# Products of constants in seven waits of TensorE: what they do to a block of four attention and feed-forward layers

## The chip, the cores and the metric

The kernel runs on one core of a Trainium2 chip. The metric is the device time of one execution in microseconds. Before the change three runs took 1488.58, 1493.6 and 1497.57 us, median 1493.6.

## The reference, cut to what matters

The reference takes x of shape (2, 1024, 256) in float32 and adds eight gated sub-layers to it, one after the other. Each reads the layer-normalised x of the one before:

```python
x = x + tanh(g_xattn[0]) * L0_xattn(layernorm(x), ctx, ...)   # A: 16 heads over 77 context rows
x = x + tanh(g_ffn[0])   * L0_ffn(layernorm(x), ...)          # B: GELU feed-forward, quantised weights, LoRA
x = x + tanh(g_xattn[1]) * L1_xattn(ctx, layernorm(x), ...)   # C: local attention
x = x + tanh(g_ffn[1])   * L1_ffn(layernorm(x), ...)          # D: windowed attention, routed heavy attention
x = x + tanh(g_xattn[2]) * L2_xattn(layernorm(x), ctx, ...)   # E: similarity x . ctx, softmax both ways
x = x + tanh(g_ffn[2])   * L2_ffn(layernorm(x), ...)          # F: gated recurrence over the 2 batch rows
x = x + tanh(g_xattn[3]) * L3_xattn(layernorm(x), ctx, ...)   # G: 16 heads again, with a bias and a mask
x = x + tanh(g_ffn[3])   * L3_ffn(layernorm(x), ...)          # H: 16 experts, 4 of them for each row
```

The change touches E, F, the start of G and H. In E the similarity of each of 2048 rows with 77 context rows goes through a softmax, weighs the context, and a second softmax over the rows gives one mean row for each of the two batches. F has two steps; the state of the first begins as a constant vector. In H a router picks 4 experts for each row, and each expert is a gated SiLU layer of 128 units.

## The kernel before, in words

Everything is float32 and stands in SBUF: x is 16 tiles of 128 rows by 256 columns, HT = 8 tiles for each of the B = 2 batches. PSUM is one tensor `ps` of 8 banks of 512 float32 values in each of 128 partitions. Each engine has one instruction stream written out by hand; semaphores order the streams. An engine works strictly in its written order, so a product that stands ahead of a wait is done whether or not the wait is over. There is no planner.

A layer ends with `x_new`: VectorE adds the layer's output to x and counts each tile on that semaphore. The next layer begins with `norm_dve` and `norm_act` (mean and variance by VectorE, the square root by ScalarE, lines 656 to 676).

Layer E on TensorE is `sim_pe`. Its steps, with the line that the profile gives each:
- It waits for E_step 1 (VectorE has made RT, line 1194) and makes a row of 154 numbers in bank 7 (line 1053).
- For n = 0 to 7, `turn_x(n)` transposes two tiles of normalised x into bank 0 or 1 (line 1063), ScalarE copies them out (line 1177), and `similarity(n)` multiplies them with RT (line 1072). VectorE takes the first four similarities at once (`largest(0)`, line 1214).
- `turn_a(0)` and `turn_a(1)` transpose the softmax weights (line 1081), ScalarE copies them (line 1185), and `weigh(0)`, `weigh(1)` multiply them with the context (line 1088).
- `from_weighed(0, b)` is lines 1098 and 1102, `batch_mean` lines 1117, 1120 and 1125, `from_x` line 1107. Then tiles 1 to 7 follow in the same way.

Layer F on TensorE is `rnn_pe`. It waits for x_new of E, though its first twelve products, one column each with a weight of 128 by 128, read only constants (line 1306). VectorE waits for them at line 1422, makes the biases and only then norms x (`norm_dve`, line 1434). `turn_x(0)` transposes four tiles (line 1321, copies line 1388), `from_x` is line 1328.

Layer G is `heads16_pe` with L = "G": after the wait for x_new of F come the keys of the context (line 298), its values (line 305), `turn_x(0)` (line 315) and `queries(0)` (line 325). VectorE spreads the keys at line 526.

Layer H is `moe_pe`. The router's tables end with products of one-hot matrices in float16 (line 2434). VectorE turns the result into addresses (line 2594), GpSimd gathers the rows of each of NJ = 80 tiles by indirect DMA (line 2676), and TensorE does for each tile `turn_rows` (line 2443), `gate_up` (line 2451), `turn_act` (line 2459) and `down` (line 2465). GpSimd's gathers of the expert outputs and the last sums follow when all 80 tiles are done.

The profile records one product of float32 matrices as two instructions MATMUL: the twelve products of line 1306 are its 24. A transposition is recorded as one.

Of the kernel before, what the change touches and what calls it, by code (L numbers as in the profile page):

```python
# [111 lines left out]
def nth(i, per, k):  # L112

    return i * per + (k + 1)
# [28 lines left out]
def done(layer, name):  # L143

    total = 0
    for each, count in TOTALS[name].items():
        if each == layer:
            return total
        total += count


def build(nc, ins, out):
    ctx = ExitStack()
    with ctx:
# [5 lines left out]
        def sem(name):  # L160
            if name not in sems:
                sems[name] = ctx.enter_context(nc.semaphore(name))
            return sems[name]
# [28 lines left out]
        packs, pk = {}, {}  # L192
# [9 lines left out]
        ps = ctx.enter_context(nc.psum_tensor("ps", [P, 8, 512], F32))  # L202
        ident = pk["const"]["ident"]
# [27 lines left out]

        block = ctx.enter_context(nc.Block())


        UNITS = [(b, c) for b in range(B) for c in range(DC)]
        NU = len(UNITS)
# [811 lines left out]
        def sim_pe(pe):  # L1048
            w = pk["E"]
            pe.wait_ge(sem("E_in"), LOADS["E"])  # L1050
            pe.wait_ge(sem("E_step"), 1)
            for c in range(DC):
                mm = nc.tensor.matmul(ps[:, 7, 0:B * SC], w["w2"][:, c:c + 1].to_broadcast([P, P]), ctxT[:, c, :],
                                      start=c == 0, stop=c == DC - 1)
            mm.then_inc(sem("E_row_ps"), 1)

            def turn_x(n):
                if n >= 2:
                    pe.wait_ge(sem("xT_ready"), nth(n - 2, 1, 0) + done("E", "xT_ready"))
                for b in range(B):  # L1060
                    pe.wait_ge(sem("xn_ready"), nth(n, B, b) + done("E", "xn_ready"))
                    for c in range(DC):
                        mm = nc.tensor.transpose(ps[:, n % 2, c * D + b * P:c * D + (b + 1) * P],
                                                 EW["xn"][:, n % 2, b, c * P:(c + 1) * P], ident)
                mm.then_inc(sem("xT_ps"), 1)
# [10 lines left out]
            def turn_a(i):  # L1076
                pe.wait_ge(sem("E_soft"), i // EHALF + 1)
                if i < 2:
                    pe.wait_ge(sem("xT_ready"), nth(HT - 2 + i, 1, 0) + done("E", "xT_ready"))
                for b in range(B):  # L1080
                    mm = nc.tensor.transpose(ps[0:SC, i % 2, b * P:(b + 1) * P], EW["sim"][:, i, b, :], ident)
                mm.then_inc(sem("aT_ps"), 1)

            def weigh(i):
                pe.wait_ge(sem("aT_ready"), nth(i, 1, 0) + done("E", "aT_ready"))
                for c in range(DC):
                    for b in range(B):
                        mm = nc.tensor.matmul(ps[:, 2 + i % 2, c * D + b * P:c * D + (b + 1) * P], ctxN[:, b, c * P:(c + 1) * P],
                                              EW["aT"][0:SC, i % 2, b * P:(b + 1) * P], start=True, stop=True)
                mm.then_inc(sem("E_hq_ps"), 1)  # L1090
# [42 lines left out]
                similarity(n)  # L1133
            turn_a(0)
            turn_a(1)
            weigh(0)
            weigh(1)
            pe.wait_ge(sem("E_taken"), 2)
# [159 lines left out]
        def rnn_pe(pe):  # L1298
            w = pk["F"]
            pe.wait_ge(sem("F_in"), LOADS["F"])  # L1300

            pe.wait_ge(sem("x_new"), NT + done("E", "x_new"))
            for g in range(3):
                for co in range(DC):
                    for ci in range(DC):
                        mm = nc.tensor.matmul(ps[:, 7, g * DC + co:g * DC + co + 1],
                                              w["u" + "fic"[g]][:, ci * D + co * P:ci * D + (co + 1) * P],
                                              w["c0"][:, ci:ci + 1], start=ci == 0, stop=ci == DC - 1)
            mm.then_inc(sem("F_u0_ps"), 1)

            def turn_x(s):
                for j in range(FJ):
                    n = s * FJ + j
                    if j == 0 and s >= 2:
                        pe.wait_ge(sem("F_ysum_ready"), (s - 1) * FJ)
                    if j:
                        pe.wait_ge(sem("xT_ready"), n + done("F", "xT_ready"))
                    for b in range(B):
                        pe.wait_ge(sem("xn_ready"), nth(n, B, b) + done("F", "xn_ready"))
                        for c in range(DC):  # L1320
                            mm = nc.tensor.transpose(ps[:, 0, c * D + b * P:c * D + (b + 1) * P],
                                                     GW["xn"][:, j, b, c * P:(c + 1) * P], ident)
                    mm.then_inc(sem("xT_ps"), 1)
# [667 lines left out]
        def route_pe(pe):  # L1991
            def prefix(v, bank):
                out_ = ps[:, bank, 0:NR].rearrange("p (g t) -> p g t", g=NG)
                nc.tensor.matmul(out_, pk["const"]["before"], v, start=True, stop=False, skip_group_check=True)
                nc.tensor.matmul(out_[:, :, 1:HT], ones, CUM[0][:, :, PAD:PAD + HT - 1], start=False, stop=True,
                                 skip_group_check=True).then_inc(sem("D_prefix"), 1)

            pe.wait_ge(sem("D_tie"), 1)
            prefix(RT["tie"], 1)
            pe.wait_ge(sem("D_sel"), 1)  # L2000
            prefix(RT["sel"], 2)
# [372 lines left out]
        XT_B, GU_B, AT_B, YT_B, LOGIT_B, RANK_B, COUNT_B, INV_B = (0, 1), (2, 3), (4, 5), (6, 7), 3, 5, 6, 7  # L2374
# [34 lines left out]
        def moe_pe(pe):  # L2409
# [15 lines left out]
                             stop=True).then_inc(sem("H_table_ps"), 1)  # L2425
# [4 lines left out]
            for t in range(NT):  # L2430
                pe.wait_ge(sem("H_hot"), t + 1)
                pe.wait_ge(sem("H_hot_scaled"), t + 1)
                for k in range(TOP):
                    mm = nc.tensor.matmul(ps[:, INV_B, 0:NJ], HOT_LO[:, t % 2, k, :], HOT_HI[:, t % 2, k, :],
                                          start=t == 0 and k == 0, stop=t == NT - 1 and k == TOP - 1)
                mm.then_inc(sem("H_inv_ps"), 1)

            def turn_rows(j):
                pe.wait_ge(sem(f"H_fetch{j // 2 % NGB}"), 32 * (j // 2 // NGB + 1))
                if j >= 2:  # L2440
                    pe.wait_ge(sem("H_xT"), j - 1)
                for c in range(DC):
                    mm = nc.tensor.transpose(ps[:, XT_B[j % 2], c * P:(c + 1) * P], FETCH_BUF[:, j % HT, c * P:(c + 1) * P], ident)
                mm.then_inc(sem("H_gT_ps"), 1)
# [26 lines left out]
            def expert(j):  # L2471
# [2 lines left out]
                    pe.load(regs[m % 2], expert_at[0:1, m * NREG:(m + 1) * NREG])  # L2474
                return pe.snap(regs[m % 2][j % NREG], min_val=0, max_val=(NE - 1) * EWID)

            pe.wait_ge(sem("H_step"), 5)
            turn_rows(0)
            at = {0: expert(0)}
# [310 lines left out]
        @block.tensor  # L2790
        def _(pe):
            heads16_pe(pe, "A")
            ffn_pe(pe)
            local_pe(pe)
            light_pe(pe)
            route_pe(pe)
            heavy_pe(pe)
            sim_pe(pe)
            rnn_pe(pe)
            pe.wait_ge(sem("x_new"), NT + done("F", "x_new"))  # L2800
            heads16_pe(pe, "G")
            moe_pe(pe)
# [112 lines left out]
```

## Time and profile before

| | |
|---|---|
| runs | 1488.58, 1493.6, 1497.57 us; median 1493.6 |
| the profiled execution | 1489.11 us, its span 1487.3 us |
| TensorE, products | 1171.2 us busy (79%), 8580 of them |
| VectorE | 907.3 us (61%) |
| ScalarE | 521.7 us (35%) |
| GpSimd | 238.5 us (16%) |
| mean granted clock of TensorE | 0.895 of full speed |

The span runs from the first to the last instruction. The granted clock of TensorE has two levels in this profile, 1.00 (2.4 GHz) and 0.50 (1.2 GHz); a stretch that shows a number between them holds some of each. Busy time of TensorE counts a product from its start to its end, and neighbours overlap, so that 100% is not the most it could do.

### The profile page before, as it was taken

The page shows a single profiled execution, that of the slowest core. Times are in us where ns is not written, and L with a number is a line of the kernel's source. Part 1 is how long each engine was busy: PE and PEld are TensorE (multiplying, and loading weights), DVE is VectorE, ACT ScalarE, POOL GpSimd, SP SyncE. Part 2 cuts the span into 40 slices and gives each one's busy share as a digit, 9 for nine tenths or more (in the row PEclk, how much of TensorE's full clock was granted, in tenths as well). Part 3 has the DMA queues.
Part 4 walks back from the last instruction along what each step waited for, and adds up shares of the span by engine and source line. Part 5 has one row for each costly group of instructions (what it writes and reads, how often), then busy time and mean ns, then how long its engine had stood idle before and what let it go on. Part 6 is the DMA issues. An engine that isn't in the chain of part 4 may idle for free.

```text
span 1487.3 us, 22658 instructions
## 1 busy us (share of the span) xinstructions
PE 1171.2 (79%) x8580; PEld 894.1 (60%) x8580; DVE 907.3 (61%) x2277; ACT 521.7 (35%) x1153; POOL 238.5 (16%) x220
## 2 busy tenths in 40 slices
PE   5988799975499988884898879899698872999500
PEld 3666588864246744662575668688476661888400
DVE  5889822157826754996363645344799976655333
ACT  2544333321227653550333321133244434444100
POOL 0009034200000010002010000000000001655376
PEclk9999999996699999997999979899799995999855
DMA  9200054300000002100000170000022102555443
GB/s 316 102 2 1 19 151 140 100 1 0 1 0 2 2 1 75 40 2 21 1 22 1 39 236 1 0 1 1 5 86 72 46 1 73 158 163 157 108 131 118
DMA packets 60001, 89.01 MB, mean 60 GB/s; under 512 B 21315, under 2 KB 50877, under 8 KB 57085
## 3 DMA queue, kind: packets, MB, share of 16 engines
q1 hardware_dynamic: 52413, 67.18, 13.9%
q0 software_dynamic: 7488, 20.46, 5.3%
q8 instruction: 68, 1.11, 0.3%
q14 instruction: 32, 0.26, 0.1%
HBM read 60.73 MB, written 26.89 MB: 59 GB/s over the span
## 4 chain that ended last, share of the span: by engine, by line
PE 53%; DVE 23%; issue 11%; ACT 6%; POOL 5%; DMA 1%; SPq 0%; DVEq 0%; POOLq 0%; ACTq 0%
PE ps L2451 5%; PE ps L1328 4%; POOL hall L2687 4%; PE ps L760 4%; PE ps L773 4%; PE ps L1833 3%; PE ps L2465 2%; DVE work L583 2%; PE ps L367 2%; PE ps L1847 2%; DVE work L574 2%; DVE work L573 2%; PE ps L1906 2%; PE ps L353 1%; PE ps L340 1%
## 5 line engine op out<-in xcount | busy, mean ns | idle before, releaser
L2676 POOL DMA_INDIRECT hall<-hall_rows,tile_idx x80 | 75.8, 948 | 423.0 <-DVE tile_idx L2594 376.0
L1768 ACT ACTIVATE work<-ps,work 128x256 f32<-128x256 f32 x128 | 58.9, 473 | 84.9 <-DVE work L1659 84.9
L340 PE MATMUL ps<-hall,work 128*128 128x308 f32 x256 | 78.8, 432 | 12.2 <-DVE work L548 5.9
L2451 PE MATMUL ps<-big,work 128*128 x320 | 84.6, 388 | 0.0
L367 PE MATMUL ps<-work,hall 78*32 78x128 f32 (+1 forms) x2048 | 69.2, 275 | 11.6 <-DVE work L584 8.5
L460 ACT COPY work<-ps 78x1024 f32<-78x1024 f32 (+1 forms) x64 | 64.3, 1005 | 38.6 <-PE ps L353 37.3
L367 PEld LDWEIGHTS ps<-work,hall 78*32 78x32 f32 (+1 forms) x2048 | 52.3, 109 | 36.1 <-ACT work L460 22.3
L353 PE MATMUL ps<-pack_const,work 128*78 128x128 f32 (+1 forms) x512 | 69.5, 279 | 3.1 <-issue 3.1
L583 DVE RECIPROCAL work<-ps 128x128 f32<-128x128 f32 x64 | 60.8, 950 | 13.8 <-PE ps L367 13.3
L2687 POOL DMA_INDIRECT hall<-expert_rows,back_idx x64 | 61.9, 967 | 39.0 <-DMA expert_rows<-work 19.8
L2649 DVE SCALAR_TENSOR_TENSOR x<-hall,work,x 128x256 f32<-128x256 f32 x64 | 31.1, 486 | 57.0 <-DMA hall<-expert_rows,back_idx 55.2
L1328 PE MATMUL ps<-work,pack_F 128*128 128x256 f32 x288 | 64.8, 385 | 0.7 <-ACT work L1388 0.7
L1833 PE MATMUL ps<-big,dpack 128*128 128x384 f32 (+1 forms) x160 | 63.3, 559 | 1.8 <-ACT big L1745 1.8
L353 PEld LDWEIGHTS ps<-pack_const,work 128*78 128x78 f32 (+1 forms) x512 | 55.7, 134 | 14.8 <-issue 11.7
L2598 DVE TENSOR_TENSOR work<-work,ps 128x128 f32<-128x128 f32 x80 | 23.2, 290 | 67.9 <-ACT work L2512 67.9
L1328 PEld LDWEIGHTS ps<-work,pack_F 128*128 128x128 f32 x288 | 55.4, 194 | 8.7 <-ACT work L1388 1.1
L340 PEld LDWEIGHTS ps<-hall,work 128*128 128x128 f32 x256 | 44.3, 192 | 24.6 <-DVE work L548 6.8
L2451 PEld LDWEIGHTS ps<-big,work 128*128 128x128 f32 x320 | 56.0, 195 | 4.8 <-issue 0.2
L760 PE MATMUL ps<-work,big 128*128 128x256 f32 x256 | 58.1, 386 | 0.7 <-ACT work L786 0.7
L773 PE MATMUL ps<-big,work 128*128 128x256 f32 x256 | 56.6, 379 | 0.0
L279 POOL TENSOR_TENSOR hall<-hall,mask_add 128x1232 f32<-128x1232 f32 x16 | 41.3, 2601 | 92.3 <-DMA hall<-in_fside 92.3
L760 PEld LDWEIGHTS ps<-work,big 128*128 128x128 f32 x256 | 49.6, 194 | 8.0 <-ACT work L786 1.1
(488 smaller groups left out, 2690.3 us busy)
## 6 DMA issues: line engine op xcount, KB each, us to landing
expert_rows<-work SPq DMA_DIRECT2D x40, 256.0 KB, 2.2
masked_bias<-hall SPq DMA_DIRECT2D x8, 1232.0 KB, 5.2
dpack<-masked_bias SPq DMA_DIRECT2D x8, 1232.0 KB, 5.9
hall<-in_fside SPq DMA_DIRECT2D x8, 616.0 KB, 7.4
dpack<-in_pack_D SPq DMA_DIRECT2D x1, 4115.0 KB, 16.3
hall_rows<-hall SPq DMA_DIRECT2D x2, 2048.0 KB, 10.5
big<-in_w SPq DMA_DIRECT2D x4, 1024.0 KB, 11.0
big<-in_pack_B SPq DMA_DIRECT2D x1, 2052.0 KB, 10.3
```

The source lines that it names most:

```text
L340: mm = nc.tensor.matmul(o, A["qT"][:, c, b * P:(b + 1) * P], KV["kbd"][:, c, b, k * 4 * SC:(k + 1) * 4 * SC], start=True, stop=True)
L353: mm = nc.tensor.transpose(ps[0:SK[L], PT_BANK + h // 4, h % 4 * P:(h % 4 + 1) * P], weights_of(L, u)[:, h, :], ident)
L367: mm = nc.tensor.matmul(ps[j * HB32:(j + 1) * HB32, 4, half:half + P], lhsT, A["pT"][0:SK[L], u % 2, h * P:(h + 1) * P], start=g == 0, sto ...
L460: nc.scalar.copy(A["pT"][0:SK[L], u % 2, :].rearrange("p (k n) -> p k n", k=2), ps[0:SK[L], PT_BANK:PT_BANK + 2, :]).then_inc(s("pT_ready" ...
L583: link(ve.reciprocal(den, DEN_REG))
L760: mm = nc.tensor.matmul(ps[:, 1 + f // 2, f % 2 * D:(f % 2 + 1) * D], w["fc"][:, c * F0 + f * P:c * F0 + (f + 1) * P], BW["xnT"][:, c, :], ...
L773: mm = nc.tensor.matmul(ps[:, 5 + b, 0:D], BW["hT"][:, f, b * P:(b + 1) * P], w["proj"][:, f * D:(f + 1) * D], start=f == 0, stop=f == FC - 1)
L1328: mm = nc.tensor.matmul(ps[:, 1 + 3 * b + g, co * FJ * P:(co + 1) * FJ * P], w[kind + "fic"[g]][:, ci * D + co * P:ci * D + (co + 1) * P], ...
L1833: mm = nc.tensor.matmul(ps[:, bank, 0:n], w["wqkv"][:, ci * 3 * HDH + col:ci * 3 * HDH + col + P], LB["xnT"][:, ci, at:at + n], start=ci = ...
L2451: mm = nc.tensor.matmul(ps[:, GU_B[j % 2], 0:2 * INTER], MW["xT"][:, j % 2, c * P:(c + 1) * P], big[:, bass.ds(at + c * 2 * INTER, 2 * INT ...
L2676: gp.indirect_dma_start(out=FETCH_BUF[:, j % HT, :], out_offset=None, in_=hall_rows[:, :], in_offset=bass.IndirectOffsetOnAxis(ap=tile_idx ...
L2687: gp.indirect_dma_start(out=hall[:, t % NGB * TOP + k, :], out_offset=None, in_=expert_rows[:, :], in_offset=bass.IndirectOffsetOnAxis(ap= ...
```

## The change

A helper `keep_busy(count, bank)` issues products of the 128 by 128 identity with a constant of 128 by 512 into one bank of PSUM. It waits for nothing and counts on no semaphore, and nothing reads what it writes. Seven calls of it are put into the stream of TensorE, 37 products in all; the other engines are not touched.

```diff
+        def keep_busy(count, bank):
+            for _ in range(count):
+                nc.tensor.matmul(ps[:, bank, :], ident, pk["const"]["slots"], start=True, stop=True)
 sim_pe:
             pe.wait_ge(sem("E_in"), LOADS["E"])
+            keep_busy(3, 1)
             pe.wait_ge(sem("E_step"), 1)
             ... the row of line 1053
             mm.then_inc(sem("E_row_ps"), 1)
+            keep_busy(2, 1)
             ... turn_x and similarity
             turn_a(0)
             turn_a(1)
+            keep_busy(6, 6)
             weigh(0)
             weigh(1)
 rnn_pe:
             pe.wait_ge(sem("F_in"), LOADS["F"])
+            keep_busy(3, 2)
             pe.wait_ge(sem("x_new"), NT + done("E", "x_new"))
             ... the twelve products of line 1306
             mm.then_inc(sem("F_u0_ps"), 1)
+            keep_busy(6, 2)
 moe_pe:
+            keep_busy(7, YT_B[0])
             pe.wait_ge(sem("H_step"), 5)
             turn_rows(0)
 the stream of TensorE:
             rnn_pe(pe)
+            keep_busy(10, 5)
             pe.wait_ge(sem("x_new"), NT + done("F", "x_new"))
             heads16_pe(pe, "G")
```

## Rows read from the trace of the kernel before

**Rows 1.** The page, part 4: the chain that ended last.

```profile
PE 53%; DVE 23%; issue 11%; ACT 6%; POOL 5%; DMA 1%; SPq 0%; DVEq 0%; POOLq 0%; ACTq 0%
```

**Rows 2.** Busy time by stretch; after POOL: granted clock, DMA share, GB/s.

```profile
847.45:851.33 3.88, 0.95 (x5) 0.56 (x4) 3.14 (x13) 0.22 (x1) 0.00 (x0) 0.99 0.38 110
851.33:861.57 10.24, 9.51 (x46) 9.26 (x46) 4.91 (x15) 2.35 (x4) 0.00 (x0) 0.50 1.10 285
...
868.72:871.81 3.09, 0.00 (x0) 0.00 (x0) 2.44 (x7) 0.48 (x2) 1.55 (x7) 0.99 1.11 338
871.81:882.05 10.24, 8.65 (x28) 7.38 (x29) 3.58 (x8) 2.04 (x5) 1.65 (x5) 0.50 0.95 360
...
940.07:943.76 3.69, 3.69 (x18) 3.60 (x17) 0.00 (x0) 0.00 (x0) 0.00 (x0) 0.50 0.00 0
943.76:947.20 3.44, 0.00 (x0) 0.00 (x0) 2.65 (x14) 0.22 (x1) 0.00 (x0) 0.50 0.00 0
...
1041.30:1045.90 4.60, 0.01 (x1) 0.00 (x0) 4.32 (x9) 2.51 (x3) 0.00 (x0) 0.99 0.00 0
...
1047.00:1052.70 5.70, 5.70 (x17) 4.29 (x18) 4.52 (x21) 0.22 (x1) 0.00 (x0) 0.50 0.00 0
...
1255.96:1261.40 5.44, 0.00 (x1) 0.03 (x1) 0.24 (x1) 0.00 (x0) 3.40 (x4) 0.50 0.17 48
1261.40:1267.75 6.35, 6.06 (x19) 4.67 (x20) 0.78 (x3) 3.19 (x7) 4.83 (x6) 0.50 0.36 106
```

**Rows 3.** Timeline of layer D: start, duration; products of 512 columns at full clock.

```profile
427.56 8.75 PE L1847 MATMUL ps<-dpack,big 128*128 128x512 f32 x20
```

**Rows 4.** Timeline of layer E, first half: turns and similarities.

```profile
852.06 1.97 PE L1063 MATMUL ps<-pack_const,work 128*128 128x128 f32 x8 [1.68 <-DVE work L1206]
...
856.28 1.82 PEld L1072 LDWEIGHTS ps<-work,hall 128*128 128x128 f32 x8
...
858.75 1.83 PEld L1072 LDWEIGHTS ps<-work,hall 128*128 128x128 f32 x8
...
862.53 0.80 DVE L1214 TENSOR_TENSOR work<-ps,work 128x616 f32<-128x616 f32 x1
862.66 0.97 PEld L1072 LDWEIGHTS ps<-work,hall 128*128 128x128 f32 x8
...
863.94 0.97 PEld L1072 LDWEIGHTS ps<-work,hall 128*128 128x128 f32 x8
```

**Rows 5.** The chain of waits through layer E: start, share of time, step.

```profile
872.46 2.09 PE ps L1088 x8
...
877.55 1.71 PE ps L1098 x4
...
895.99 0.87 PE ps L1098 x4
...
901.17 0.89 PE ps L1088 x8
```

**Rows 6.** The same chain: one-column products, and the start of layer F.

```profile
886.62 1.07 PE ps L1125 x8
...
939.23 4.54 PE ps L1306 x24
...
950.79 12.04 PE ps L1328 x48
...
964.59 10.36 PE ps L1328 x48
```

**Rows 7.** Timeline of the start of layer G.

```profile
1052.69 0.86 DVE L526 SCALAR_TENSOR_TENSOR hall<-ps,dpack,pack_const 128x616 f32<-128x616 f32 x1
```

**Rows 8.** Timeline of layer H: gate and up products of tiles 1, 4 and 5.

```profile
1264.93 1.91 PE L2451 MATMUL ps<-big,work 128*128 x4
...
1270.75 1.03 PE L2451 MATMUL ps<-big,work 128*128 x4
...
1272.37 1.03 PE L2451 MATMUL ps<-big,work 128*128 x4
```

## The prediction

> **What bounds the kernel now.** I read the chain of waits first: more than half of the span runs through TensorE, a quarter through VectorE [rows 1], so what TensorE does sooner in the right places shortens the kernel. Then I read the stretches with their granted clock. They show why a wait of TensorE costs more than its own length. After the last products of D the engine has only the short row of line 1053 to do, 0.95 us in 3.88, and the clock goes from 1.00 to 0.50; the next 10.24 us, in which it has work for 9.51, pass at half clock. It goes the same way behind the idle 3.09 us ahead of `weigh(0)` (10.24 us at half clock follow), in the one-column products of F, behind the idle 4.60 us ahead of G, and H starts its 80 tiles at half clock for 6.35 us [rows 2]. Since the clock and not the data sets the pace there, these stretches are what the change can win. It can win them only where TensorE's end is awaited, and only if it doesn't itself come late.
>
> **What one added product costs.** The trace has products of the same size: 20 records of 128x512 in 8.75 us at full clock, and the last ends some 0.6 us after it starts, so 0.43 us from one to the next [rows 3]. A product is two records, so 0.86 us at full clock and 1.71 at half. The 37 cost 31.7 us at full clock. The waits they stand in were, in order, 1.98, 1.68, 3.74, 1.59, 3.45, 5.69 and 5.44 us (TensorE's idle time as the trace has it before lines 1053, 1063, 1088, 1306, 1321, 298 and 2443; the longer ones are the stretches of [rows 2]), together 23.6. So the products overrun the waits by 8 us and more, and each place is a sum of two terms: how late the awaited work starts, and what full clock gives back behind it. The Trainium skill, page "TensorE: Matmul & The Clock Gate", section Back-to-back issue gap, gives 216 ns for 512 columns at the high clock, for bf16. By that price the 37 products would take 8.0 us, never overrun, and the ten ahead of G would fill 2.2 us of 5.69. The trace contradicts it for this data: 0.43 us a record and two records a product, four times as much.
>
> **Layer E, first half (3 and 2 products).** The last product of D starts at about 847.4. Three take 2.57 us: 850.0. The row of line 1053 takes some 0.55 (850.6), two more 1.71: 852.3. `turn_x(0)` began at 852.06 [rows 4], so it is 0.25 us late. Then it pays back: from one similarity to the next it was 2.47 us at half clock (856.28 to 858.75) and 1.28 at full (862.66 to 863.94) [rows 4]. The clock came back only at 861.57 [rows 2]. At full clock eight transpositions are done at about 853.3, ScalarE's copy is there at 853.5, four similarities with their turns take 4 x 1.28 = 5.1 and some 0.5 for the first copies: 859.2, where VectorE took them at 862.53 [rows 4]. That is 3.3 us. VectorE's own work for the later tiles follows at its own pace and moves as a whole. I take **-3.3**. Bounds: 4 x 1.19 = 4.8 gained if nothing is late, and 0 if VectorE sets this half alone.
>
> **Layer E, second half (6).** Six take 5.14 us behind `turn_a(1)`, which ended at about 868.6: free at 873.8, where `weigh(0)` began at 872.46 [rows 5]: 1.3 us late. Behind it, from 872.46 to the end of the sixteen records of lines 1098 and 1102, TensorE took until 883.27. At full clock: 1.06 for the eight of line 1088 (in steady tiles 0.89 [rows 5]), about 1.0 for ScalarE's two copies, 1.06 again, and 16 records at 0.87/4 = 3.5, where they took 1.71/4 each at half [rows 5]: 6.6 in place of 10.8 us. Net 1.3 - 4.2 = -2.9; some is lost if the clock sags between the two `weigh`: **-2.8**. Bounds: -4.2 and +1.3. What is late next is the same chain, the mean row of each batch through VectorE; the idle time behind it is not filled and stays as it is.
>
> **Layer F (3 and 6).** Three from 937.45 end at 940.0; x_new let line 1306 start at 939.23 [rows 6], so 0.8 late. Its 24 records took 4.54 us, 0.19 each at half clock, and eight like them took 1.07 at full, 0.13 each [rows 6]: 3.1 us, end 943.1 in place of 943.8. VectorE's biases and norm, which wait for that end, take 3.4 us on their own: 946.5. But six products from 943.1 end at 948.25: `turn_x(0)`, which started at 947.21, is now 1.05 late, held by the added products alone. From there to the end of the first 48 records of line 1328 it was 15.6 us, and at full clock it is 12.85: two turns at 0.63, two copies at 0.6, and 10.36 as in the second step, where the first took 12.04 [rows 6]. Net -1.7 if the clock holds. It may not: in the one-column products the clock stood at 0.50 to their end though weight loads were busy 3.60 of 3.69 us [rows 2]. If it falls in them again, some of the six run at half clock, up to 1.7 us more, and the net is 0. I take **-1.2**. Bounds: -2.8, and +5.4 with all six at half clock (10.3 us) and their later gain kept.
>
> **Start of G (10).** From 1041.2 at full clock ten take 8.57: 1049.75, where line 298 began at 1047.0. Keys then take 1.1 and values 1.75 us at full clock: 1052.6, as before (all of it was at half clock [rows 2]). VectorE spreads the keys at 1052.69 [rows 7], since it is occupied by its own norm and memsets until then. The late start and the clock cancel: **-0.1**. Bounds: -1.0 and +2.7.
>
> **H (7).** Here the clock is at half when they start, at 1256.0, and the gathers let line 2443 begin at 1261.40. How soon does work bring the clock back? Twice the trace shows it from a standstill: 5.70 us from 1047.00, 6.35 us from 1261.40 [rows 2]; in F it came 2.94 us after 950.79, with two turns ahead of that. I take 4.8: 2.8 products, then 4.2 at full clock, 3.6 us: the end is 1264.4, 3.0 late. At full clock the way to tile 1's `gate_up`, 3.53 us, loses about 1.4, and from there to tile 4's 5.82 us become 3 x 1.62 = 4.86 [rows 8]. Net 3.0 - 1.4 - 0.96 = **+0.6**. Bounds: -0.9 and +4.3 (all seven at half clock, 12.0 us, end 1268.0). All behind it, the other tiles and the last gathers, moves by the net.
>
> **The sum.** -3.3 - 2.8 - 1.2 - 0.1 + 0.6 = -6.8 on 1489.11: 1482.3 (the span's 1487.3 with the 1.8 us around it, less 6.8) for an execution whose clock falls where the profiled one's did. The median of the runs is 4.5 us above it. I read that spread as the clock's own, since where it falls and comes back relative to the work can't be fixed by the program; part of it lies in the five places. So the likeliest median lies between 1482.3 and 1493.6 - 6.8 = 1486.8: **1485 us**, 0.6% below 1493.6.
>
> **The rivals.** (a) *The products overrun more than they win.* For: 31.7 us in 23.6 us of waits, the one-column products, and a half clock at the start of H. F gives 0 and H +1.5: -4.7 in all, 1487 (with the forecast's 2.7 us for the median, as in the next two). (b) *VectorE holds layer E.* The gain of its first half comes to nothing, -3.5 in all, 1488. Against: VectorE stood waiting for line 1063 before each of its norms there. (c) *The products don't hold the clock*, since they are constants or come too late for it. Then each call is pure delay at half clock, counted from where the clock fell before: +1.4 and +3.4 in E (six end at 875.9), +7.5 in F (ten and more us for six, end 954.7), +6.6 in G, +6.7 in H: 25.6 us slower, 1517. It decides from the point where a call is longer than its wait, which at half clock is nearly everywhere. Against: transpositions with the identity, constants as well, stood in stretches at full clock. A mild form, in one layer only, is inside the range. (d) *Other executions lose more than the profiled one* in the five places, 1.6 us more in each, 14.8 in all off the median of 1493.6: 1479. For: the clock came back in F 2.94 us into line 1328, the soonest of all.
>
> **How the numbers follow.** Forecast 0.48 (its own range 1481 to 1489), (a) 0.25, (b) 0.10, (c) 0.05, (d) 0.12. Range 1478 to 1492. The bound for a difference is 0.5%, here 1486.1, about what a measurement of this kernel can tell. Two thirds of the forecast lie below it, all of (d) and a third of (a): faster 0.53. The rest but for (c): same 0.42. Slower 0.05.
>
> **What would show it.** Step by step: no half clock between 847 and the end of the first similarities, and line 1214 some 3 us sooner behind the last product of D; line 1088 starting right behind the added products, and line 1098 at 0.22 us a record; line 1306 done in about 3 us; line 1321 of F starting right behind the six; line 526 of G unmoved against the end of F; line 2443 held past the landing of its rows by about 3 us, and the clock at 1.00 there. The forecast is wrong if an added record takes much more or less than 0.43 us, or if the clock falls in spite of them.

## The result, and the profile after

The changed kernel takes 1486.88 us (median of 20 runs, 1481.24 to 1491.55); the kernel before takes 1493.55 (median of 20 beside them, 1486.12 to 1499.47). The ratio is 0.9955, with a 95% interval of 0.994 to 0.997: 6.7 us faster, a gain that is real and small, 0.45%. The forecast was 1485.0 us. The profiled execution of the changed kernel took 1486.32 us, its span 1484.5.

The page first: span, busy time and the chain's shares. The 37 products are there as 74 more MATMUL records than before (8654 against 8580).

```profile
span 1484.5 us, 22804 instructions
...
PE 1193.2 (80%) x8654; PEld 898.1 (61%) x8654; DVE 916.6 (62%) x2277; ACT 521.7 (35%) x1153; POOL 237.4 (16%) x220
...
PE 59%; DVE 24%; ACT 6%; issue 5%; POOL 5%; DMA 1%; DVEq 0%; SPq 0%; POOLq 0%; ACTq 0%
```

TensorE's share of the chain rises from 53% to 59% and "issue" falls from 11% to 5% [rows 1]. That is no gain in itself: the added products stand on the chain where waits stood.

Then the stretches that answer to [rows 2]: start and end, length, busy time and instructions of PE, PEld, DVE, ACT and POOL, then granted clock, DMA share and GB/s.

```profile
851.70:858.00 6.30, 6.21 (x25) 3.34 (x23) 5.45 (x20) 1.06 (x3) 0.00 (x0) 1.00 0.59 187
858.00:868.90 10.90, 10.37 (x93) 9.94 (x93) 8.47 (x19) 5.69 (x9) 0.00 (x0) 1.00 1.17 281
868.90:874.00 5.10, 5.10 (x14) 2.23 (x14) 3.06 (x9) 1.08 (x3) 1.61 (x7) 1.00 1.19 296
874.00:886.18 12.18, 9.18 (x77) 7.05 (x75) 5.13 (x12) 1.81 (x4) 1.04 (x4) 1.00 0.99 364
886.18:893.01 6.83, 5.39 (x17) 4.67 (x18) 3.94 (x9) 0.00 (x0) 0.00 (x0) 0.50 0.00 1
937.40:940.80 3.40, 3.40 (x27) 3.06 (x26) 0.46 (x3) 0.00 (x0) 0.00 (x0) 1.00 0.00 0
940.80:944.21 3.41, 3.41 (x5) 1.35 (x4) 2.81 (x14) 0.22 (x1) 0.00 (x0) 0.50 0.00 0
...
1038.50:1047.10 8.60, 8.60 (x22) 3.82 (x21) 7.58 (x21) 2.73 (x4) 0.00 (x0) 1.00 0.00 0
1253.10:1258.24 5.14, 5.14 (x10) 2.21 (x8) 0.24 (x1) 0.00 (x0) 3.08 (x3) 0.50 0.17 51
1258.24:1261.70 3.46, 3.46 (x9) 1.47 (x8) 0.00 (x0) 0.00 (x0) 2.63 (x3) 1.00 0.37 99
```

Layer E runs at 1.00 from D's last product to 886.18, where it had spent two stretches of 10.24 us at 0.50. In F the clock still falls, but 3.4 us later and in the added products. The products ahead of G hold it. Those ahead of H begin at half clock and it comes back 5.1 us into them.

The timeline of TensorE: L238 is the added product, L1070 to L1124 are layer E, L1315 and L1331 F, L303 G's keys, L2453 and L2461 `turn_rows` and `gate_up` of H (before: 1063 to 1117, 1306, 1321, 298, 2443, 2451).

```profile
851.71 2.74 PE L238 MATMUL ps<-pack_const 128*128 128x512 f32 x6
...
856.52 1.19 PE L1070 MATMUL ps<-pack_const,work 128*128 128x128 f32 x8
...
859.19 1.01 PE L1079 MATMUL ps<-work,hall 128*128 128x77 f32 x8
...
860.48 1.01 PE L1079 MATMUL ps<-work,hall 128*128 128x77 f32 x8
...
868.85 5.32 PE L238 MATMUL ps<-pack_const 128*128 128x512 f32 x12
874.00 1.06 PE L1095 MATMUL ps<-work,ctxN 77*128 77x128 f32 x8
876.00 1.16 PE L1095 MATMUL ps<-work,ctxN 77*128 77x128 f32 x8 [0.94 <-ACT work L1193]
876.99 1.03 PE L1105 MATMUL ps<-pack_E,work 128*128 128x256 f32 x4
877.86 1.03 PE L1109 MATMUL ps<-pack_E,work 128*128 128x256 f32 x4
...
937.40 2.73 PE L1315 MATMUL ps<-pack_F 128*128 128x1 f32 x24
...
940.00 7.09 PE L238 MATMUL ps<-pack_const 128*128 128x512 f32 x12
...
946.93 0.60 PE L1331 MATMUL ps<-pack_const,work 128*128 128x128 f32 x4
...
1038.49 8.75 PE L238 MATMUL ps<-pack_const 128*128 128x512 f32 x20
...
1047.07 1.22 PE L303 MATMUL ps<-ctxT,dpack 128*128 128x154 f32 x8
...
1253.14 8.78 PE L238 MATMUL ps<-pack_const 128*128 128x512 f32 x14
1261.76 0.60 PE L2453 MATMUL ps<-pack_const,hall 128*128 128x128 f32 x4
...
1268.55 1.03 PE L2461 MATMUL ps<-big,work 128*128 x4
```

The similarities of [rows 4] now start 1.29 us apart where they had been 2.47 us apart at half clock. `weigh(0)` begins right behind the twelve records, and the next product of E comes 0.87 us after the first of its kind where that had taken 1.71 [rows 5]. In F twelve records take 7.09 us, 1.8 us more than E's twelve at full clock (5.32). The twenty ahead of G take 8.75, to the hundredth what [rows 3] gave for twenty.

**Between the same instructions in every trace.** I took the starts (or ends) of the same instructions in each kernel's trace and subtracted them. Stage figures below come from this table (us), or were read in the same way from the traces that it leaves out. The kernels other than "before" and "after" are described further on; "FGH only" has the products of F, G and H alone, "gaps" is the changed kernel with other counts and places.

```
                                    before  after E only FGH only trimmed u0 early moved  gaps gaps,F hold F
start to D's last product           847.64 851.87 852.82  847.13  856.41  858.63 857.02 854.35 849.63 854.46
D's last product to largest(0)       14.89  10.94  10.95   14.68   10.94   10.94  15.67  10.95  10.95  10.94
largest(0) to weigh(0)                9.93  11.18  11.18    9.94    9.93   11.18  10.19  11.18  11.18  11.18
weigh(0) to first mean product       10.74   6.54   6.54   10.62    8.32    6.54   9.44   6.54   6.54   6.54
E's first from_x to E's last product 47.36  47.37  47.15   47.30   46.85   47.06  47.13  44.76  44.76  44.76
E's end to second turns of F         25.02  25.01  26.70   25.01   22.48   20.13  20.49  19.86  25.00  19.01
F's end to keys spread (G)           11.38  11.38  11.38   11.38   11.38   11.38  11.38  11.38  11.38  11.38
keys spread to queries(0) copied      3.27   3.13   2.32    3.12    0.78    3.12   2.01   0.78   0.78   0.77
queries(0) to H's ranks             172.24 172.43 171.13  172.42  173.79  173.91 178.66 171.16 178.49 169.68
H's router end to turn_rows(0)        5.44   8.41   5.42    8.39    5.61    8.23   5.51   5.48   5.48   5.44
turn_rows(0) to gate_up of tile 4     9.35   6.79  12.28   12.05   12.99   12.20  11.63  13.15   8.19   8.16
from there to H's last product      125.47 125.17 129.25  125.89  126.80  127.63 129.56 127.23 125.16 125.20
```

Column "before" against "after", stage by stage: D to `largest(0)` -3.95; E's second half +1.25 and -4.20; F's start 0.0; G 0.0 and -0.14; H +2.97 and -2.56. That is -6.6; with what is left behind it the time from D's end falls by 7.0. The first row tells why the two profiled executions differ by only 2.8 us (1489.11 and 1486.32): the code ahead of E is the same in both, and it took 4.23 us longer in the second.

How much of a row is one execution's own? A second trace of the changed kernel has the rows from D's end to the mean product and the start of F to 0.01 us. It has 171.49 us from `queries(0)` to the ranks where the first has 172.43, and 11.92 from `turn_rows(0)` to tile 4 where the first has 6.79.

### The profile page after: what moved, and what is told of

Its sections match the earlier page's. It is cut to its first block, busy times and chain, and to the rows that moved or that the text cites. A ratio compares the mean times of both kernels' runs of the same rounds, so it can differ in the third digit from the quotient of the medians.

```text
span 1484.5 us, 22804 instructions
## 1 busy us (share of the span) xinstructions
PE 1193.2 (80%) x8654; PEld 898.1 (61%) x8654; DVE 916.6 (62%) x2277; ACT 521.7 (35%) x1153; POOL 237.4 (16%) x220
## 4 chain that ended last, share of the span: by engine, by line
PE 59%; DVE 24%; ACT 6%; issue 5%; POOL 5%; DMA 1%; DVEq 0%; SPq 0%; POOLq 0%; ACTq 0%
PE ps L2461 5%; PE ps L1338 4%; POOL hall L2698 4%; PE ps L778 4%; PE ps L765 4%; PE ps L1843 3%; PE ps L238 2%; PE ps L2475 2%; DVE work L588 2%; PE ps L1857 2%; PE ps L372 2%; DVE work L579 2%; DVE work L578 2%; PE ps L1916 2%; PE ps L345 1%
## 5 line engine op out<-in xcount | busy, mean ns | idle before, releaser
L2461 PE MATMUL ps<-big,work 128*128 x320 | 82.6, 381 | 0.3 <-ACT work L2519 0.3
L2461 PEld LDWEIGHTS ps<-big,work 128*128 128x128 f32 x320 | 54.6, 190 | 4.8 <-issue 0.6
## 6 DMA issues: line engine op xcount, KB each, us to landing
hall_rows<-hall SPq DMA_DIRECT2D x2, 2048.0 KB, 10.3
```

Source lines behind the costliest of these rows:

```text
L2461: mm = nc.tensor.matmul(ps[:, GU_B[j % 2], 0:2 * INTER], MW["xT"][:, j % 2, c * P:(c + 1) * P], big[:, bass.ds(at + c * 2 * INTER, 2 * INT ...
```

## The experiments

They ran in three sets, each on one chip with runs of the kernel before beside them: E only, F+G+H, trimmed and u0 early (before: 1500.5 us); the changed kernel again, gaps, gaps without H, and moved (before: 1501.2); gaps with F as changed, hold F, and moved again (before: 1495.55). Ratios are to the kernel before of the same set, with 95% intervals; they are taken from all runs of both kernels and need not be the quotient of the two medians. The theory going in: all of the gain is E's; the products of F, G and H pay for themselves at best, because they come late by as much as the clock gives back. Rival: F, G or H carry part of it, or cost and are covered by E.

**The changed kernel again (e0_after).** No edit.

> The changed kernel itself, for comparison on the same chip as the next three. Theory and rival both: ratio to before 0.994 to 0.997.

Measured 1493.83 us, ratio 0.9952 (0.9926 to 0.9977): the first result's ratio, at other absolute times.

**E's products alone (e1_E_only).**

```diff
-            keep_busy(3, 2)      # F, ahead of x_new
-            keep_busy(6, 2)      # F, behind the one-column products
-            keep_busy(7, YT_B[0])
-            keep_busy(10, 5)
```

> Keeps the three calls in layer E (3, 2 and 6 products) and leaves out the four in F, G and H. Theory: all of the change's gain sits in E. From the last product of D to line 1102/1109's end the stage is some 6.9 us shorter than in the kernel before (4.0 in the first half, 2.9 in the second), while F, G and H come back to their old lengths; median about 1487, within 1 us of the whole change. Rival: the calls in F, G and H carry a part of the gain in most executions, by half-clock stretches that the one profiled execution happened not to show; then this kernel is 2 us or more slower than the whole change, 1489 or more.

**F's, G's and H's alone (e2_FGH_only).**

```diff
-            keep_busy(3, 1)
-            keep_busy(2, 1)
-            keep_busy(6, 6)
```

> Leaves out the three calls in E and keeps F (3 and 6), G (10) and H (7). Theory: nothing is won. F's step is 0 to -1.7 us by where the clock falls in the one-column products, G's is 0 within 0.3, H's +0.4: the median is within 1.5 us of the kernel before. Rival (they carry a part): 2 us or more faster than before.

Measured 1494.31 us, 0.995 (0.9924 to 0.9976), and 1502.21 us, 1.0005 (0.9982 to 1.0028). E's eleven products carry the gain, and the other 26 together show none; by the interval they can be worth 2.7 us at most, or cost 4.2. The stages have the same from D's end to the mean product, 28.67 us with E only and 28.66 with the whole change, where the kernel before has 35.56 and F+G+H 35.24.

One stage does not fit the expectation that F comes back to its old length. With E only its start takes 26.70 us, 1.7 more than in the kernel before (25.02), which has no added product there either: the half clock lasted 17.07 us here and 13.65 there. The four traces with the calls of 3 and 6 (both of the change, F+G+H, and one further on) all have 25.00 or 25.01. So those calls neither win nor lose against the one trace of the kernel before, and win 1.7 us against this one.

**Shorter calls (e3_trimmed).** The calls that the trace after shows to hold their awaited work.

```diff
-            keep_busy(6, 6)
+            keep_busy(4, 6)
-            keep_busy(3, 2)
+            keep_busy(2, 2)
-            keep_busy(6, 2)
+            keep_busy(4, 2)
-            keep_busy(7, YT_B[0])
+            keep_busy(4, YT_B[0])
-            keep_busy(10, 5)
+            keep_busy(6, 5)
```

> The whole change with fewer products where the trace shows them still running when the work behind them was ready: E's third call 6 to 4, F 3 to 2 and 6 to 4, G 10 to 6, H 7 to 4. Theory: the overrun is paid in full and the clock needs no more than these. Against the whole change weigh(0) starts 1.3 us sooner after turn_a(1), F's turn_x(0) 1.5 or more sooner after E's end, line 303 of G 2.7 sooner and VectorE's wait for the queries of G 2 us shorter, H's first turn_rows 2 to 3 sooner; together 5 to 7 us, a median of 1480 to 1482. Rival: the overrun is hidden behind VectorE and the gathers, or the shorter calls let the clock fall, so that the median stays at 1485 or above.

Measured 1490.06 us, 0.9928 (0.9901 to 0.9956). I had expected 5 to 7 us less than the whole change; the ratios differ by about 4 us and their intervals overlap, so the totals don't show the trimmed version to be faster. The stages show where it is. F's start is 2.5 us shorter and G's queries come 2.35 sooner. But four products in E are too few. The timeline and the two stretches behind:

```profile
873.38 3.60 PE L238 MATMUL ps<-pack_const 128*128 128x512 f32 x8
877.28 1.16 PE L1095 MATMUL ps<-work,ctxN 77*128 77x128 f32 x8 [0.31 <-ACT work L1193]
...
880.79 1.91 PE L1105 MATMUL ps<-pack_E,work 128*128 128x256 f32 x4
```

```profile
876.47:879.88 3.41, 2.16 (x14) 1.47 (x13) 1.32 (x5) 1.61 (x4) 0.22 (x2) 1.00 1.11 311
879.88:883.29 3.41, 3.41 (x12) 2.93 (x12) 1.60 (x3) 0.58 (x1) 0.00 (x0) 0.51 1.09 353
```

`weigh(0)` starts when its data are there and not 1.25 us late, but TensorE is busy only 2.16 us of the next 3.41 and the clock falls behind them: 8.32 us instead of 6.54. Between these traces the late start of six was worth its price, by 0.5 us.

**The one-column products ahead of the wait (e4_u0_early).** They read constants only, so they need not wait for x_new; one product of 512 columns stands in their middle, four behind them.

```diff
-            keep_busy(3, 2)
-            pe.wait_ge(sem("x_new"), NT + done("E", "x_new"))
+                    (in the loop) if n_u0 == 3: keep_busy(1, 2)
-                        mm = nc.tensor.matmul(ps[:, 7, g * DC + co:g * DC + co + 1],
+                        mm = nc.tensor.matmul(ps[:, 0, g * DC + co:g * DC + co + 1],
-            keep_busy(6, 2)
+            keep_busy(4, 2)
```

> The whole change, but the twelve one-column products of F go ahead of the wait for x_new (into bank 0, free by then) with one product of constants in their middle, and 4 products behind them in place of 3 ahead and 6 behind. Theory: F's step failed because the clock fell in the one-column products and because VectorE waits for them. Here the clock stays at 1.00 from E's end to F's first line 1338, VectorE's wait for them falls from 3.8 us to under 1.5, and F's turn_x(0) starts about 9 us after E's last product in place of 12: 2.5 to 3.5 us faster than the whole change, about 1484. Rival: F's start is bound by VectorE's norm anyway and this moves by less than 1 us.

Measured 1490.11 us, 0.9918 (0.9887 to 0.9948), in the stage 20.13 us where the change has 25.01. The timeline of F's start, TensorE and VectorE:

```profile
941.28 1.39 PE L1317 MATMUL ps<-pack_F 128*128 128x1 f32 x12
...
943.48 1.40 PE L1317 MATMUL ps<-pack_F 128*128 128x1 f32 x12
...
945.01 0.17 DVE L1434 TENSOR_TENSOR work<-ps,pack_F 128x6 f32<-128x6 f32 x1 [2.12 <-PE ps L1317]
...
948.33 0.76 PE L1333 MATMUL ps<-pack_const,work 128*128 128x128 f32 x4
```

VectorE still waited 2.12 us for them (I had expected less than 1.5) and the first turn was possible 6.9 us behind E (I had expected 9). Here the clock stays at 1.00 through the narrow products and behind them. The four behind them are not what held it, for the trimmed kernel has four as well and its clock fell; whether the product in the middle did it or the earlier place is not separated. The total is again not told apart from that of the whole change.

**Moved work, no constants (e6_moved_work, e10_moved_again).** The kernel before, with F's one-column products ahead of the wait and VectorE's norm ahead of its biases, so that nobody waits for them. This asks whether F's start needs any added product at all.

```diff
-            pe.wait_ge(sem("x_new"), NT + done("E", "x_new"))      # TensorE, F
-   u0 into ps[:, 7, ...]
+   u0 into ps[:, 0, ...]
             dve.wait_ge(sem("F_in"), LOADS["F"])
+            norm_dve(dve, "F")
             dve.wait_ge(sem("F_u0_ps"), 1)
...
-            norm_dve(dve, "F")
             normed(0)
+            (the three small bias operations, then E_step 7, for which ScalarE waits)
```

> The kernel before with no product of constants at all, but with work moved into a wait: the twelve one-column products of F go ahead of the wait for x_new, and VectorE norms x first and makes the biases behind it (ScalarE waits for them). Theory: the order, not the clock, was the larger cost at the start of F. VectorE no longer waits 4.8 us for these products nor spends 0.8 on the biases first: from E's last product to F's first turn_x some 4.5 us in place of 9.6, though all of it at or near half clock; about 5 us faster than before. Rival: TensorE's half clock behind the wait grows by what is saved, and the gain is under 2 us.

> The kernel with moved work and no product of constants, once more: its stage was 4.5 us shorter in the trace and its median not different from before. Theory: the work's place is worth 3 to 5 us and the first set of runs was met by falls of the clock elsewhere, as in its trace at the end of G: 0.997 here. Rival: 0.9998 again, so that what it saves at the start of F is lost somewhere that the milestones must show.

Measured 1501.57 us, 0.9998 (0.9977 to 1.0019), and again 1490.62 us, 0.9986 (0.9967 to 1.0005). In the stage both traces have the gain: 20.49 and 20.6 us in place of 25.02. The totals show none. Moving alone still leaves one wait of TensorE, now for the norm:

```profile
946.37 3.02 PE L1305 MATMUL ps<-pack_F 128*128 128x1 f32 x24
...
950.72 1.12 PE L1320 MATMUL ps<-pack_const,work 128*128 128x128 f32 x4 [1.33 <-DVE work L1431]
```

In the traces of the moved kernel 6.4 us are lost again 260 us further on, in code that no kernel here touches. Stretches at the end of layer G, of the moved kernel and then of the changed kernel on the same chip:

```profile
1211.53:1214.94 3.41, 3.41 (x17) 3.18 (x15) 1.98 (x5) 0.98 (x2) 0.00 (x0) 0.51 0.02 5
1218.36:1231.10 12.74, 12.74 (x59) 12.27 (x57) 2.92 (x11) 4.90 (x7) 0.00 (x0) 0.50 0.00 0
```

```profile
1217.80:1222.70 4.90, 4.90 (x46) 4.82 (x45) 2.32 (x10) 2.84 (x4) 0.00 (x0) 1.00 0.01 3
```

TensorE is fully busy in all three and the clock is at half in the first two. What runs there are transpositions and the products of 16 columns of H's gate, here eight records of the latter at either level:

```profile
1220.30 1.73 PE L2402 MATMUL ps<-dpack,pack_F 128*128 128x16 f32 x8
```

```profile
1218.25 0.96 PE L2411 MATMUL ps<-dpack,pack_F 128*128 128x16 f32 x8
```

From `queries(0)` to the ranks of H the moved kernel took 178.66 us, and 178.65 in its second trace; the kernel before took 172.24. "Gaps, F as changed" has it too (178.49). "Trimmed" and "u0 early" have the first of the two stretches and only 3.41 us of the second, and take 173.79 and 173.91.

This is not chance alone. In the nine traces of kernels without products inside G the clock falls once more right behind `queries(0)`, and how long behind them orders the whole stage (us):

```
                      E only  again  before  FGH only  after  trimmed  u0 early  moved  moved again
queries(0) to fall      5.97   6.69    6.95      7.04   7.11     8.02      8.27   9.07         9.13
queries(0) to ranks   171.13 171.49  172.24    172.42 172.43   173.79    173.91 178.66       178.65
```

("again" is the second trace of the changed kernel.) So the loss depends on where the clock's changes stand against G's work, and the place can be read 150 us before the loss is paid. The two traces of the moved kernel agree in that place to 0.06 us, on two chips and with 10 us between their starts of E, so the shift of the work seems to set it. What the clock follows there is not shown.

The totals don't tell how often it happens. The profiled execution of the second set of runs has the loss and is, with 1488.30 us, the fastest of its twelve. A gain of 4.5 us would be a ratio of 0.997, which the first interval excludes and the second just holds.

**All gaps filled by what the trace says is idle (e5_all_gaps).** The changed kernel with counts that fit the waits and four further calls in E and G.

```diff
             E: 3, 2 and 6 as before
+                keep_busy(1, 2)      # ahead of the wait for E_step 5
+            keep_busy(2, 2)          # ahead of the wait for E_step 6
             F: one-column products and norm moved as in the kernel above, one product
                in their middle; the calls of 3 and 6 are gone
-            keep_busy(10, 5)
+            keep_busy(6, 5)
+                    keep_busy(2, 5)  # G, tile 0, ahead of scores(0, 2)
+                    keep_busy(2, 5)  # G, tile 0, ahead of turn_p(0, 0)
-            keep_busy(7, YT_B[0])
+            keep_busy(3, YT_B[0])
```

> Both together, with calls by the measured waits: E 3, 2 and 6 as in the change, and 1 and 2 more in the two waits around line 1132; F as in the kernel with moved work, with one product of constants in the middle; G 6 in place of 10, and twice 2 ahead of its waits in tile 0; H 3 in place of 7. Theory: against the whole change E's waits around the mean row keep the clock at 1.00 (fx0 to E's end 2.6 us shorter), F's start is 7 us shorter, G's first queries come 2.3 us sooner and its second half-clock stretch of 10.2 us goes (2 to 3 us), H 1: 13 to 17 us faster than the whole change, some 20 faster than before. Rival: what is won in one place is lost again to new falls of the clock elsewhere (as four products in E did), and it is less than 8 us faster than the whole change.

**The same without H's three (e7_all_gaps_no_H).**

```diff
-            keep_busy(3, YT_B[0])
```

> The same without the three products ahead of the experts of H. Theory: the gathers and the half clock there share the wait, so that from the last one-hot product to the fifth tile's gate_up it is 0 to 2 us longer than with three, and the median differs by less than 2 us. Rival: the products delay the first tile by as much as they win, and it is the same or faster without them.

Measured 1483.1 us, 0.9884 (0.9858 to 0.9909), and 1484.22 us, 0.989 (0.9859 to 0.9921), beside the changed kernel's 1493.83 on the same chip: 10.7 us better than the change, where I had expected 13 to 17. The three products of H make no difference that can be told. E's second part is 2.6 us shorter (44.76) and F's start 5.1 us (19.86), where I had expected 7.

**Gaps, but F's start as in the change (e8_gaps_F_as_changed).** The kernel of "all gaps" with the waits, the calls of 3 and 6 and the order of VectorE's work in F put back.

```diff
+            keep_busy(3, 2)
+            pe.wait_ge(sem("x_new"), NT + done("E", "x_new"))
...
+            keep_busy(6, 2)
```

> The kernel with all gaps (1 and 2 more products in E, 6 at the start of G and twice 2 behind, 3 in H), but with the start of F as the change has it: 3 products, the wait for x_new, the twelve one-column products, 6 products, and VectorE's old order. Theory: moved work in F is worth the 5 us that the traces show from E's end to F's second turn (25.0 in the whole change, 19.9 with all gaps), so this is 4 to 6 us slower than with all gaps, about 0.9915 of before. Rival: as in the kernel with moved work alone, it shows in the stage and not in the total: 0.989.

**All gaps, and the clock held through F's copies (e9_hold_F).**

```diff
                     if j:
+                        if s == 0:
+                            keep_busy(1, 2)
                         pe.wait_ge(sem("xT_ready"), n + done("F", "xT_ready"))
...
             turn_x(0)
+            keep_busy(1, 2)
             pe.wait_ge(sem("xT_ready"), FJ + done("F", "xT_ready"))
```

> The kernel with all gaps and two products more, one in each of F's two waits for ScalarE's copy (0.68 us each) behind its first transpositions. There the clock fell in spite of the product in the middle of the one-column products. Theory: the clock stays at 1.00, the stage from F's first turn to its second shortens from 15.6 us to 13.4 less than 0.4 us of overrun: 2 us faster than with all gaps, about 0.987. Rival: they only overrun, and it is the same or slower.

Measured 1485.01 us, 0.9937 (0.9916 to 0.9957), and 1473.16 us, 0.9842 (0.9818 to 0.9867). The first was expected 4 to 6 us slower than all gaps. The ratios (0.9937 and 0.9884, of different sets) say some 8; the start of F has 5.1 of them, and its trace has the loss in G. The second has the lowest median here, 22 us below the kernel before on its chip, and its interval lies wholly below that of the change, while it overlaps that of all gaps (0.9858 to 0.9909). F's start tells the two apart by 6.0 us in the stage (25.00 and 19.01); in the traces the end of G tells them apart by another 8.8 (178.49 and 169.68), which is the matter above. The code ahead of E took 4.8 us longer in the second trace, so that the stages don't add up to the 11.9 us between the medians. The timeline of F's start in the second kernel, and its clock:

```profile
937.01 1.40 PE L1321 MATMUL ps<-pack_F 128*128 128x1 f32 x12
939.18 0.76 PE L1338 MATMUL ps<-pack_const,work 128*128 128x128 f32 x4 [0.78 <-DVE work L1450]
939.78 1.65 PE L238 MATMUL ps<-pack_const 128*128 128x512 f32 x2
941.23 1.06 PE L1338 MATMUL ps<-pack_const,work 128*128 128x128 f32 x4
942.08 1.71 PE L238 MATMUL ps<-pack_const 128*128 128x512 f32 x2
```

```profile
936.00:940.00 4.00, 3.23 (x21) 2.52 (x22) 3.38 (x14) 0.23 (x2) 0.00 (x0) 1.00 0.00 0
940.00:943.40 3.40, 3.40 (x8) 1.68 (x7) 1.59 (x8) 1.15 (x2) 0.00 (x0) 0.51 0.00 0
```

Against "all gaps", which had half clock here over 6.80 us:

```profile
939.20:946.00 6.80, 5.45 (x16) 3.93 (x17) 2.59 (x10) 1.17 (x2) 0.00 (x0) 0.50 0.00 0
```

Two products halve the stretch but do not prevent it; the stage is 0.85 us shorter, where I had expected 2. The step from 0.9884 to 0.9842 is six us, and this accounts for less than one; the rest is not explained by the two products.

## Why the prediction was right, and which step failed

The time (1485.0 against 1486.88) and the sum from D's end (-6.8 against -7.0) were right; not every term was. That the sum fits so well is partly luck: E's first half gave 0.65 us more than forecast, G and H 0.2 more together, E's second half 0.15 more, and F 1.2 less.

**One product.** Right: twenty records in 8.75 us at full clock, 0.43 from one to the next. The Trainium skill's 216 ns (page "TensorE: Matmul & The Clock Gate", section Back-to-back issue gap) is for bf16, and no trace here has such a product; a count made from it would have been four times too many for each wait.

**E, first half, -3.3.** Right in kind, short in size: -3.95. The start was as forecast: `turn_x(0)` 4.65 us behind D's last product where it had been 4.42, so 0.23 late (forecast 0.25). The term that was too small is what full clock gives back from there to `largest(0)`: 10.47 us became 6.29, 4.2 us and not 3.6. Rival (b), that VectorE holds the layer, falls with it.

**E, second half, 1.3 late and 4.2 back.** +1.25 and -4.20: right term by term. I took 0.1 off for a sag between the two `weigh`, and the clock did not sag there. That "E only" has the whole ratio (0.995), and F+G+H none of it, shows that E's two terms are the result.

**F, -1.2.** This is the step that failed: 0.0. Its term was how late the six products let F's first turn start. The forecast was 1.05 us late and 2.75 back; measured were 2.37 late (11.94 us behind E's end in place of 9.57) and 2.38 back. The prediction named the branch ("if it falls in them again ... the net is 0") and gave the better one more weight. The one-column products did take about 3 us as forecast (2.73), then the clock fell at 940.80, 0.8 us into the added products, and six of them took 7.09 us and not 5.32. F's first turn was held by them and by nothing else: VectorE's normalised tiles were there from 943.5 on, the turn began at 946.93. The clock fell there in all five traces that have the 24 one-column records behind added products, between 0.2 us before and 0.9 us behind their end. So the narrow products just ahead are the likely cause of the fall, though no run changes them alone. In the kernel "u0 early", where they stand ahead of the wait for x_new with one product of 512 columns among them, the clock stayed, and 4.9 us came off the stage. The forecast called itself wrong if the clock fell in spite of the added products; in F it did, for 3.41 us.

Its upper bound doesn't come out of its terms either. Six products from 943.1 in 10.3 us end 6.2 us late, and with the gain of 2.75 kept that is +3.4, not +5.4. Nothing else used it.

**G, -0.1.** 0.0 to the keys, -0.14 to the queries. Right: ten are a late start that full clock repays. Six give the queries 2.35 us sooner than ten, and the change left these. Against the kernel before six are worth 1.2 to 2.5 us, since without any product this stage took 3.27, 2.32, 2.01 and 2.08 us in four traces.

**H, 3.0 late, net +0.6.** 2.97 late, 2.56 back, +0.41. This compares one trace with one, and the experiments of the first two sets can't confirm it. All eight of their traces, with and without products, have a stop that the other five lack: 7 to 15 us behind `turn_rows(0)` TensorE stands still once or more, the longest time for 1.9 to 3.3 us. In the second trace of the changed kernel:

```profile
1273.63 1.13 PE L2461 MATMUL ps<-big,work 128*128 x4 [1.98 <-issue]
```

What stops it is not shown. In the five traces without it, the time from the router's end to `gate_up` of tile 4 is 14.79 and 14.43 us with no product, 15.20 with seven, 13.67 and 13.60 with three. So seven cost about 0.4 us there and three win about 1. Three are nearly free of a late start (5.48 and 5.44 in place of 5.44).

**The median.** I read the 4.5 us between the profiled execution and the median as the clock's, falling elsewhere. The first row of the table agrees with a large spread in unchanged code, which took from 847.13 to 858.63 us in the traces, both on one chip. The forecast was 1.9 us too low; it let 1.8 us of that spread lie in the five places, and the measured difference of the medians, 6.7 us, gives no sign of it. The reading that the place of the clock's falls can't be fixed by the program was too strong: in the nine traces in which it falls there, the next fall in E begins 48.8 to 49.4 us before the end of E's last product, though the code ahead of E took up to 11.6 us more or less.

**The chances.** I put 0.53 on a gain of over 0.5%. It came to 0.45%, inside the "same" to which I gave 0.42. Rival (a), F 0 and H too late, 1487 us, is near what happened, nearer than the forecast; rival (c), that constants don't hold the clock, fell with the granted clock of 1.00 from 851.70 to 886.18. Rival (d) predicted more than was there.

## What to carry to other kernels

Products that nobody reads can hold TensorE's clock through a wait (1.00 from 851.70 to 886.18 here), but each is an instruction in front of the awaited one: measure one (here 0.86 us), divide the measured wait by it, and prefer one too many only where a long chain at half clock stands behind (six in E, not six in F). Look first for real work that can stand in the gap, as F's twelve products did, then fill the rest. Judge by the stage and by the total: a gain in a stage is not kept for sure, since a shift of the work also shifts it against the clock's changes, and the price can come 260 us later. One trace of the kernel before is a thin base for such a comparison: its F stage was 25.02 us, and 26.70 in a second kernel with the same code there.

## What was not expected of the hardware

- Layer E's transpositions and products of 77 columns keep the clock at 1.00 (858.00 to 868.90, weight loads busy 9.94 of 10.90 us) once it is there, and at 0.50 they left it there for 10.24 us [rows 2]. The same work ran at both levels; what differed was what came just ahead of it.
- Products of one column don't hold it though TensorE shows no idle time: busy 3.40 of 3.40 us at 1.00, weight loads 3.06, then 0.50. With one product of 512 columns between the two halves and four behind them it stayed in one trace; in three others, where turns and waits follow the halves, it fell 0.9 to 1.6 us behind them.
- A fall can come behind the stretch in which TensorE had gaps: in the trimmed kernel the clock is 1.00 while TensorE is busy 2.16 of 3.41 us, and 0.51 in the next 3.41, in which it is busy throughout.
- TensorE can be at half clock with work without a gap: 12.74 of 12.74 us busy at the end of G with products of 16 columns and transpositions, in three of thirteen traces; in the others most or all of this work ran at 1.00. It cost 6.4 us, as much as the whole change brings. In the two of the three without products in G the fall behind `queries(0)` stood 9.1 us behind them, and not 6 to 7 as in the five that lost nothing.
